# The first layer's keys and values: second steps side by side in two 64-row tiles, and the keys' product at the end of the cycle

## The reference, cut to what matters

```python
x = x + _L0_xattn_ref(_layernorm(x), ctx_768, mask, Wq, Wk, Wv, Wo)   # 16 heads of 16
# q = norm(x) @ Wq;  k = context @ Wk;  v = context @ Wv     Wk, Wv: 192 x 256
# out = softmax(q k^T * 0.25, masked) v @ Wo
x = x + _L0_ffn_ref(...)    # each row is routed to one of 8 experts
x = x + _L1_xattn_ref(...)  # the same context, its own Wk, Wv
x = x + _L1_ffn_ref(...)    # six cells of multi-head attention
```

## Time and profile before

| what | value |
|---|---|
| median of 3 runs | 4046.48 us (4045.95 to 4048.25) |
| profiled execution | 4048.74 us, span 4046.9 us |
| TensorE busy | 3974.8 us, 98% of the span |
| ScalarE busy | 2651.8 us, 66% |
| VectorE busy | 2400.2 us, 59% |
| GpSimd busy | 1865.0 us, 46% |
| mean granted clock of TensorE | 0.995 |

### The profile page before, as it was taken

How to read it: one execution, slowest core, us unless ns; L and a number is a source line. 1 busy time by engine, 2 the same in 40 slices (tenths; PEclk the granted TensorE clock), 3 DMA queues, 4 the chain that set the end, 5 groups by cost and what they waited for, 6 DMA issues and landing times.

```text
span 4046.9 us, 100880 instructions
## 1 busy us (share of the span) xinstructions
PE 3974.8 (98%) x38276; PEld 3397.6 (84%) x38276; DVE 2400.2 (59%) x6216; ACT 2651.8 (66%) x11851; POOL 1865.0 (46%) x1979
## 2 busy tenths in 40 slices
PE   8999999999999999999999999999999999999998
PEld 6888876678888888888888888888888888888887
DVE  6888861025566666656666666566666656656654
ACT  8998961125666666666666666666666666666765
POOL 5788872113444444444444444444444444444434
PEclk9999999999999999999999999999999999999999
DMA  3232214520000000000000000000000000000000
GB/s 103 75 105 76 72 52 154 168 78 18 12 14 15 15 14 14 13 17 15 14 13 13 14 13 13 19 13 12 13 12 12 12 12 12 12 12 12 7 4 9
DMA packets 117867, 129.74 MB, mean 32 GB/s; under 512 B 12006, under 2 KB 110676, under 8 KB 117264
## 3 DMA queue, kind: packets, MB, share of 16 engines
q1 hardware_dynamic: 105648, 109.80, 8.5%
q0 software_dynamic: 6144, 8.43, 0.7%
q10 hardware_dynamic: 5600, 5.07, 0.4%
HBM read 89.68 MB, written 41.94 MB: 33 GB/s over the span
## 4 chain that ended last, share of the span: by engine, by line
PE 76%; DVE 1%; ACT 0%; POOL 0%; issue 0%; DMA 0%; POOLq 0%
PE c_product L1552 37%; PE c_product L1563 15%; PE c_product L1611 10%; PE c_scores L1601 7%; PE c_product L1634 5%; PE c_product L1622 2%; DVE c_qT L1407 1%; PE c_product L1540 1%; ACT c_front_probs L1364 0%; PE c_product L1671 0%; DMA out<-c_fin 0%; POOL c_fin L1348 0%; DVE c_nodes L1407 0%; POOL c_front_probs L1318 0%; ACT c_probsT L1370 0%
## 5 line engine op out<-in xcount | busy, mean ns | idle before, releaser
L1318 POOL TENSOR_TENSOR c_probs<-c_probs,c_row_inv 128x512 f32<-128x512 f32 x744 | 770.3, 1045 | 1357.0 <-DVE c_row_inv L1419 1351.4
L1364 ACT ACTIVATE c_probs<-c_scores,c_neg_max 128x128 f32<-128x128 f32 x2976 | 1052.6, 407 | 333.1 <-DVE c_neg_max L1416 332.9
L1552 PE MATMUL c_product<-c_nodes,cell_w 128*128 128x256 f32 x4352 | 1065.2, 383 | 2.8 <-DVE c_nodes L1478 2.4
L1552 PEld LDWEIGHTS c_product<-c_nodes,cell_w 128*128 128x128 f32 x4352 | 796.2, 190 | 121.4 <-DVE c_nodes L1407 8.3
L1416 DVE TENSOR_REDUCE c_neg_max<-c_scores 128x4 f32<-128x512 f32 x1024 | 658.9, 680 | 177.6 <-PE c_scores L1601 170.1
L1364 ACT ACTIVATION_READ_ACCUMULATOR c_probs<-c_scores,c_neg_max 128x1 f32 x2976 | 733.1, 246 | 0.0
L1370 ACT COPY c_probsT<-c_product 128x512 f32<-128x512 f32 x744 | 408.1, 602 | 433.9 <-PE c_product L1611 430.4
L1364 ACT ACTIVATE c_front_probs<-c_scores,c_neg_max 128x128 f32<-128x128 f32 x1120 | 399.6, 398 | 182.5 <-DVE c_neg_max L1416 182.5
L1563 PE MATMUL c_product<-cell_w,c_nodes 128*128 128x256 f32 x1792 | 429.3, 379 | 0.0
L1318 POOL TENSOR_TENSOR c_front_probs<-c_front_probs,c_row_inv 128x512 f32<-128x512 f32 x280 | 295.0, 1057 | 291.0 <-DVE c_row_inv L1419 289.3
L474 ACT ACTIVATE a_probs<-a_scores,a_neg_max 128x128 f32<-128x128 f32 x1024 | 360.4, 409 | 47.4 <-DVE a_neg_max L545 47.0
(11 more groups left out here) (181 smaller groups left out, 6449.7 us busy)
## 6 DMA issues: line engine op xcount, KB each, us to landing
e_w<-in_L_ffn_w SPq DMA_DIRECT2D x12, 1024.0 KB, 6.2
a_x<-in_x SPq DMA_DIRECT2D x32, 256.0 KB, 3.0
a_ctxT<-in_ctx_pairsT SPq DMA_DIRECT2D x32, 256.0 KB, 3.5
x<-a_x SPq DMA_DIRECT2D x32, 256.0 KB, 2.1
xn<-a_xn SPq DMA_DIRECT2D x32, 256.0 KB, 2.2
c_routed<-xn SPq DMA_DIRECT2D x32, 256.0 KB, 2.7
c_x<-x SPq DMA_DIRECT2D x32, 256.0 KB, 3.1
c_ctxT<-in_ctx_pairsT SPq DMA_DIRECT2D x32, 256.0 KB, 2.8
```

The lines of the kernel that those rows point to most:

```text
L1318: nc.gpsimd.tensor_tensor(e, e, rinv[:, i, r].unsqueeze(2).broadcast_to([P, 4, T]), ALU.mult).then_inc(norm_made, 1)
L1364: a = nc.scalar.activation(probs(n, j)[:, r, k], S[r][:, k], ACT.Exp, bias=nmax[:, i, r, k:k + 1], accum_out=rsum[:, i, r, k:k + 1])
L1552: i = T_.matmul(m[:, u], w[:, k, u * P:(u + 1) * P], src[:, k], start=n == 0, stop=n == last)
```

## The change

K moves in TensorE's cycle from between r.n and O to between Tx and V. There K of job j and V of job j - 1 are joined: first the two full steps of K, then the two of V, then the second steps of both in turns: K's in array rows 0 to 63, V's in rows 64 to 127, into two banks. VectorE's K^ moves behind V^. In memory the last 64 rows of the context stand twice instead of once with zeros, and Wv has its last 64 rows behind the gap of 64 zero rows instead of ahead of it. The second layer computes from the same arrays with full steps as before. ScalarE's and GpSimd's lists are as they were.

```diff
 FIRST_PE_ORDER = """
-Tn:6 Q:1 T0.1:3 T1.1:3 S0:1 A:3 r.n:7 K:0 O:3 T1.0:2 T0.0:2 S1:1 L:6 Tx:0 V:1
+Tn:6 Q:1 T0.1:3 T1.1:3 S0:1 A:3 r.n:7 O:3 T1.0:2 T0.0:2 S1:1 L:6 Tx:0 K:0 V:1
 """
 FIRST_DVE_ORDER = """
-O^:3 S1.i3:2 st1:3 S0.i1:1 S0.i3:1 S0.i0:1 S0.i2:1 S1.x3:1 S1.x2:1 S1.x1:1 Tx^:0 L^:6 S1.x0:1 r.sh:6 V^:1
-Tn^:5 Q^:0 r.oh:6 S1.i1:1 S1.i0:1 st:-1 S0.x2:0 S0.x0:0 S0.x3:0 A^:2 r.n^:6 S1.i2:1 S0.x1:0 mk:-2 K^:-1
+O^:3 S1.i3:2 st1:3 S0.i1:1 S0.i3:1 S0.i0:1 S0.i2:1 S1.x3:1 S1.x2:1 S1.x1:1 Tx^:0 L^:6 S1.x0:1 r.sh:6 V^:1 K^:0
+Tn^:5 Q^:0 r.oh:6 S1.i1:1 S1.i0:1 st:-1 S0.x2:0 S0.x0:0 S0.x3:0 A^:2 r.n^:6 S1.i2:1 S0.x1:0 mk:-2
 """
 FIRST_PE_HEAD = """
-K:0 Tx:0 Q:0 S0:0 Tx:1 V:0 K:1 Q:1 S1:0 Tx:2 K:2 S0:1 V:1 T0.0:0 T1.0:0 S1:1 Q:2 T0.1:0 T1.1:0 S0:2 A:0 V:2
+K:0 Tx:0 Q:0 S0:0 Tx:1 K:1 V:0 Q:1 S1:0 Tx:2 K:2 S0:1 V:1 T0.0:0 T1.0:0 S1:1 Q:2 T0.1:0 T1.1:0 S0:2 A:0 V:2
...
                 elif n == "K":
...
+                    if after != ("V", j - 1):
+                        project(product(n, j), wk, ct[:, o]).then_inc(prod, 1)
+                    else:
+                        keys_m = product(n, j)
+                        for u in range(2):
+                            T_.matmul(keys_m[:, u], wk[:, 0, u * P:(u + 1) * P], ct[:, o, 0], start=u == 0, stop=False)
                 elif n == "V":
...
+                        for b in range(PAIR):
+                            T_.matmul(m[:, b], ct[:, o, 0, b * T:(b + 1) * T], wv[:, 0], start=b == 0, stop=False)
+                        for u in range(2):
+                            k = T_.matmul(keys_m[:, u], wk[half[0], 1, u * P:(u + 1) * P], ct[half[0], 1 - o, 1], start=False, stop=u == 1)
+                            v = T_.matmul(m[:, u], ct[half[1], o, 1, u * T:(u + 1) * T], wv[half[1], 1], start=False, stop=u == 1)
+                        k.then_inc(prod, 1)
+                        v.then_inc(prod, 1)
...
+    arrays["ctx_pairsT"] = np.ascontiguousarray(np.concatenate([c, c[:, P:]], 1))
...
+        arrays[n + "_Wk_rows"] = np.concatenate([wk, gap])
+        arrays[n + "_Wv_rows"] = np.concatenate([wv[:P], gap, wv[P:]])
```

More of the change, by code:

```diff
@@ L151 @@
 S0.i1:3 S0.i2:2 S0.i0:3 V^:3 O^:1 st1:1 S1.x0:3 S1.x1:3 Tx^:4 S1.x3:3 K^:4 S1.x2:3 Q^:4 S0.i3:3 st:5 S1.i1:3
-S1.i3:3 S0.x0:4 S0.x1:4 S1.i2:3 S0.i2:3 S0.x3:4 S1.i0:3 A^:2 S0.x2:4 K^:5 S0.i0:4 O^:2 st1:2 S0.i3:4 S0.i1:4
+S1.i3:3 S0.x0:4 S0.x1:4 S1.i2:3 S0.i2:3 S0.x3:4 S1.i0:3 A^:2 S0.x2:4 S0.i0:4 O^:2 st1:2 S0.i3:4 S0.i1:4
 """
@@ L689, in project_rows @@
                 return i
-            for n, j in on_pe:
+            keys_m = None
+            half = slice(0, P // 2), slice(P // 2, P)
+            for (n, j), after in zip(on_pe, on_pe[1:] + [None]):
                 o = j % 2
@@ L747, in _ @@
                     pe.wait_ge(wk_in, 16)
-                    project(product(n, j), wk, ct[:, o]).then_inc(prod, 1)
+                    if after != ("V", j - 1):
[4 more added lines that the diff above has]
+                            T_.matmul(keys_m[:, u], wk[:, 0, u * P:(u + 1) * P], ct[:, o, 0], start=u == 0, stop=False)
                 elif n == "V":
@@ L751, in _ @@
                     pe.wait_ge(wv_in, 16)
-                    project_rows(product(n, j), wv, ct[:, o]).then_inc(prod, 1)
+                    m = product(n, j)
+                    if keys_m is None:
+                        project_rows(m, wv, ct[:, o]).then_inc(prod, 1)
+                    else:
+                        for b in range(PAIR):
[5 more added lines that the diff above has]
+                        v.then_inc(prod, 1)
+                        keys_m = None
                 elif n == "O":
@@ L1741 @@
           "L1_ffn_Wo", "L1_ffn_ln_g", "L1_ffn_ln_b"]
-def whole_tiles(a, axis):
-    pad = [(0, -a.shape[i] % P if i == axis else 0) for i in range(a.ndim)]
-    return np.ascontiguousarray(np.pad(a, pad))
 def lay_out(inputs):
@@ L1752, in lay_out @@
     c = arrays.pop("ctx_768")
[L1753 to L1756, removed]
+    c = c.reshape(-1, PAIR, *c.shape[1:]).transpose(0, 3, 1, 2).reshape(c.shape[0] // PAIR, c.shape[2], PAIR * c.shape[1])
+    arrays["ctx_pairsT"] = np.ascontiguousarray(np.concatenate([c, c[:, P:]], 1))
+    for n in ("L0_xattn", "L1_xattn"):
+        wk, wv = arrays.pop(n + "_Wk"), arrays.pop(n + "_Wv")
+        gap = np.zeros_like(wk[P:])
+        arrays[n + "_Wk_rows"] = np.concatenate([wk, gap])
+        arrays[n + "_Wv_rows"] = np.concatenate([wv[:P], gap, wv[P:]])
     arrays["mask_BxS2_bf1"] = np.ascontiguousarray(inputs["mask_BxS2_bf1"]).view(np.uint8)
```

## The result

| | before | after |
|---|---|---|
| median | 4046.22 us (4 runs) | 4075.11 us (4074.81 to 4075.84, 4 runs) |
| ratio | | 1.0071 (95% interval 1.0054 to 1.0089) |
| profiled execution, span | 4048.74, 4046.9 us | 4074.89, 4073.1 us |

The change costs 28.9 us by the medians and 26.2 us between the two spans (the profiled execution of before was longer than all four of its runs). Predicted were +21.7 us, 4068, in a range of 4048 to 4082, with 0.75 for slower.

What follows compares the result with a forecast made beforehand. It took TensorE's work and ScalarE's chain to xn as bounds; 21 plain cycles at +0.85 us (+17.9) and six routing cycles at +0.64 (+3.8) gave +21.7, 4068 us on the median, range 4048 to 4082.

Steps and rivals of the forecast that it cites:

- What bounds: First layer: TensorE and ScalarE both close to full; ScalarE's chain to xn has 0.32 us to spare at Tx.
- The small tiles: Joined K and V: 64-row pairs run side by side, 2.80 us together, saving TensorE 0.66 us a cycle.
- The wait at O: Between A and O: without K, TensorE waits 0.88 us for A's eviction; O starts 3.98 after S0.
- Tx: Start of Tx in plain cycles: waits 0.63 us for xn, starts 10.31 after S0, a gain of 0.32 only.
- Tx to S0: Stretch from Tx to the next S0: 1.07 us longer plus 0.1 waiting at the banks, 7.38 instead of 6.21.
- Plain cycle: Cycle without a routing step: 17.69 us against 16.84, +0.85 us, 21 times, +17.9.
- Routing cycle: Cycle with a routing step: chain 0.2 late, Tx at 13.89, net +0.64 us, six times, +3.8.
- The count: Sum over the first layer's 27 cycles: 17.9 us plain and 3.8 us routing, +21.7 us.
- The head: Written head, K of job 1 beside V of job 0: taken at nothing, at most 0.7 us gained.
- The tiles side by side: Joined K and V: two 64-row tiles overlap; rival without overlap, 23 us more, 4091, chance 0.08.
- A's eviction alone: Rival: only the wait before O counts, Tx at 9.7, plain cycle +0.24 us, 4052, chance 0.13.
- TensorE alone: Rival: TensorE sets the cycle, both waits vanish, 0.66 us saved each, 18 us faster, 4028.5, chance 0.10.

Runs made afterwards that it cites:

- full-steps kernel: The changed kernel with K and V again in four full steps each, one product after the other, so only K's move is left: 4091.34 us, ratio 1.0107.
- fourth experiment: The changed kernel with xn two copies earlier in ScalarE's list and L moved between A and O: 4053.78 us, ratio 1.0016.

## Why the prediction was right, point by point

- **What bounds.** Right in the plain cycles: two chains end close together, TensorE's own work and S0, maxima, exponentials, copies, xn, Tx; the change lengthens the part that follows the second. Shown by the rows after (Tx 0.05 us behind xn) and by the three experiments that move xn and L.
- **The small tiles.** Right in kind, 0.09 us short in size: 2.89 for 2.80 us. The first of the four passes holds the array 0.32 us (316.45 to 316.77) instead of 0.216. The loss that I had weighed by the Trainium skill (TensorE: Matmul & The Clock Gate, Measured speedup vs the span model), pairs of 1.12 us, is close to the 1.07 from 316.45 to 317.52; but that holds the gap at the end, and the three later passes show no loss. So its sum (4075) came out nearer than mine, for another reason.
- **The wait at O.** Right: O at 3.99 for 3.98.
- **Tx.** Right: 10.32 for 10.31. On the way the S1 round took 1.44 us instead of 1.22, since its mask products met the last exponentials; it was hidden by the wait for xn.
- **Tx to S0.** The term that was mis-sized: 7.61 us (321.75 - 314.14) for 7.38. Of the 0.23, K and V have 0.09, Tn 0.05 (0.49 for 0.44), Q with the wait for K's eviction 0.04 (1.87 for 1.83), the transposes 0.03 (1.87 for 1.84), Tx 0.02. Over 27 cycles that is 6 us.
- **Plain cycle.** +1.08 for +0.85.
- **Routing cycle.** 21.3 to 21.5 us, for 21.26: right in size by luck. I had xn ready at 13.84 after S0 and Tx waiting for it. In all six it was ready at 13.2, and Tx, at 13.73 to 13.87, waited for TensorE's own chain, in which O ran at about half the clock (last section). Two errors offset each other. In the full-steps kernel, whose lists are the same, two routing cycles ran without the fall:

```profile
413.54 1.99 PE L688 MATMUL a_product<-a_wo,a_oT 128*128 128x256 f32 x8 [2.67 <-DVE a_oT L570]
...
420.35 0.66 PE L674 MATMUL a_product<-consts_sb,a_xn 128*128 128x128 f32 x4 [0.16 <-ACT a_xn L487]
```

There Tx stands 13.23 behind S0 (407.12), right behind xn. With the changed kernel's 7.59 from Tx to S0 that would be 20.8 us, an estimate: +0.2 by my mechanism instead of +0.64, and the rest is the clock. That xn came 0.46 earlier than before, where I had said 0.2 later, goes back to one routing instruction of VectorE, which took 0.79 us in most routing cycles of before and 0.23 after (last section); the chain's start did move later, by 0.12 us.
- **The count.** From Q of job 4 to Q of job 31 the kernels drift apart by 25.3 us, of the spans' 26.2. 21 plain cycles at 1.08 would give 22.7 and six routing ones at 0.87 5.2, together 27.9. It is less by 2.7, because seven plain cycles of before were longer than 16.84, by 0.06 to 0.65 (2.9 in all), and after it one by 0.19. So from my 21.7: 4.8 more for the plain cycles, 1.4 for the routing ones, 0.7 for the head, 0.2 behind it all, and 2.7 less for the long cycles of before, which I had not counted. That the sum missed by only 4.5 us of 26.2 owes something to their opposite signs.
- **The head** gave no gain but cost 0.7 us. K of job 2 now waits 4.7 us for K's eviction, where 3.4 were spent on V's. It starts 0.6 us earlier all the same (28.65 for 29.28), but behind the longer wait the low clock lasts longer: S0 of job 1 takes 2.18 us at a granted clock of 0.53, where it took 1.22 at 1.00. The seven profiles with this head have S0 of job 4 at 81.5 to 82.7 us, the two with the old one at 80.9.
- **The rivals.** The tiles side by side are shown; A's eviction alone is refuted by L's move; TensorE alone did not set the cycle in any order with K moved; in the kernel before, whose plain cycles hold no wait, it does, and the early xn is without effect there.

## What to carry to other kernels

Before work is moved within a cycle, write for each part of it between two joins (here S0 to Tx, Tx to S0) which chains run across it; work taken from a part where another engine's chain is nearly as long frees only the difference (0.3 of 1.7 us), and in the part where it arrives it counts in full. A long wait in a profile is worth what stands behind it: the one at O, 0.8 us in every cycle, could be filled without any effect until xn came earlier. A product between two others can be the cover of an eviction, as K was for A's and V for that of Tx: ask for each step removed what waited behind its back.

## What the runs showed of the hardware

Two 64-row float32 tiles in separate PSUM banks stream side by side (starts 0.01 us apart, 0.22 us a pass as for a full tile); the first pass after the change of shape takes 0.32 us.

VectorE's routing product L619 (a_exp times a_mx) took 0.79 to 0.80 us in four of the six routing cycles of before, where GpSimd's normalisation, L427, had started about 0.4 us ahead of it; it ended about 0.1 us behind that instruction each time. It took 0.23 in the other two, where L427 was over or ended within its first 0.12 us, and 0.22 to 0.23 in all six after, with GpSimd idle:

```profile
307.80 1.07 POOL L427 TENSOR_TENSOR a_probs<-a_probs,a_row_inv 128x512 f32<-128x512 f32 x1
308.16 0.79 DVE L619 TENSOR_TENSOR a_gate_probs<-a_exp,a_mx 128x64 f32<-128x64 f32 x1
```
```profile
321.32 0.23 DVE L619 TENSOR_TENSOR a_gate_probs<-a_exp,a_mx 128x64 f32<-128x64 f32 x1
```

The routing chain starts 1.03 us ahead of S0 before and 0.91 after. The two no longer meet, which takes about 0.56 us out of that chain in four cycles; I had overlooked it. With the pair between A and O they meet worse: there L619 takes 1.48 us in five of six routing cycles, which last 21.17 us and more, and 0.22 in the sixth, which lasts 19.90. This is read from the traces; no run moves GpSimd's step alone.

In the routing cycles the wait at O is now 2.67 us, where it was at most 1.18, with a second wait of 1.38 at the transposes behind O, all at a granted clock of 1.00. Now the clock fell at the wait's end in all six routing cycles, to 0.51 to 0.54 over O; windows of the changed kernel (window, busy us, clock, DMA share, GB/s), the wait and then O:

```profile
325.50:328.17 2.67, 0.01 (x1) 0.00 (x0) 2.63 (x7) 1.81 (x11) 2.41 (x6) 0.95 0.00 0
328.17:331.55 3.38, 3.38 (x9) 2.65 (x9) 2.65 (x8) 3.06 (x18) 2.93 (x3) 0.53 0.00 0
```

O took 3.38 us at 0.53, near the lower of the two levels, 1.2 of 2.4 GHz, instead of 1.83. In the kernel with xn earlier the same wait stands ahead of O with no fall:

```profile
322.30:325.05 2.75, 0.08 (x1) 0.00 (x1) 2.72 (x8) 1.81 (x11) 2.49 (x6) 1.00 0.00 0
325.05:326.90 1.85, 1.85 (x9) 1.59 (x10) 1.75 (x5) 1.85 (x12) 1.85 (x2) 1.00 0.00 0
```

There that routing cycle lasts 20.5 us, and four with a fall 21.5: about 1 us each. In the changed kernel all six had the fall and lasted 21.3 to 21.5. In the one of the windows:

```profile
333.80 1.13 ACT L487 ACTIVATE a_xn<-a_x,a_shift,a_rstd 128x256 f32<-128x256 f32 x2
...
335.52 0.64 PE L674 MATMUL a_product<-consts_sb,a_xn 128*128 128x128 f32 x4
```

xn is ready at 333.80 + 1.13 = 334.93 and Tx starts at 335.52, so the fall can have cost at most 0.5 us there, some 3 us in six. This was not tried by itself, but the full-steps kernel bears it out: its two routing cycles without a fall last 21.47 us, its four with one 21.90 to 22.13. A fall does not need a wait of 2.67 us: with L moved, O waited 1.82 us, and three of six routing cycles had one; in the kernel with Tn moved too it waited 1.67, and all six had one. What decides it stays open.

Whether the wider scatter of the fourth experiment (4051.69 to 4062.09) comes from these falls stays open; its longest execution, the profiled one, is mostly longer elsewhere. It spends 3493.3 us behind S0 of job 31, where the other eight profiles have 3483.8 to 3490.0; its three cycles with a fall are 0.6 to 1.8 us longer than the three without, 3.0 us together.
